# A causal mask moved from TensorE matmuls into VectorE's score maxima, in the first of four attention stages of a ten-stage network

## The reference, cut to what matters

```python
Q = (X @ W_q).reshape(b, n, H, 2 * DH).transpose(0, 2, 1, 3)   # H = 8, DH = 16, n = 256
Q1, Q2 = (Q[..., :DH], Q[..., DH:])                            # K1, K2 likewise
causal = jnp.tril(jnp.ones((n, n), jnp.bool_))
A1 = jnp.where(causal, jnp.einsum('bhqd,bhkd->bhqk', Q1, K1) * scaling, neg_inf)
A2 = jnp.where(causal, jnp.einsum('bhqd,bhkd->bhqk', Q2, K2) * scaling, neg_inf)
attn = softmax(A1, axis=-1) - lam * softmax(A2, axis=-1)
O = jnp.einsum('bhqk,bhkd->bhqd', attn, V)                     # then RMS norm, W_o, residual
```

## Time and profile before

| | |
|---|---|
| runs, us | 2519.81, 2519.93, 2523.47 |
| profiled execution, span, us | 2522.1 |
| busy, us | PE 2226.5, DVE 1726.6, ACT 1597.0, POOL 1213.1 |
| first attention stage, 30 to 437 us | 407.0: PE busy 403.0, DVE 298.8, ACT 266.5, POOL 233.2, granted TensorE clock 1.00 |

### The profile page before, as it was taken

How to read it: one execution, slowest core, us unless ns; L and a number is a source line. 1 busy time by engine, 2 the same in 40 slices (tenths; PEclk the granted TensorE clock), 3 DMA queues, 4 the chain that set the end, 5 groups by cost and what they waited for, 6 DMA issues and landing times. The chain is left out here.

```text
span 2522.1 us, 59734 instructions
## 1 busy us (share of the span) xinstructions
PE 2226.5 (88%) x19192; PEld 1631.9 (65%) x19192; DVE 1726.6 (68%) x4756; ACT 1597.0 (63%) x3564; POOL 1213.1 (48%) x1722
## 2 busy tenths in 40 slices
PE   8999998899699887999779888899698788888996
PEld 5666665699466655799666555589444455555795
DVE  6677776444578786544667888666788577886666
ACT  5666665377466665577548888544476178886444
POOL 4456665455244555455123566456411234665563
PEclk9999999899799999999879999899897989998998
DMA  8100000322300001222200000223300000001225
GB/s 284 63 6 12 13 12 11 102 67 71 80 2 6 16 15 53 79 70 64 71 5 2 9 17 18 71 67 82 97 1 1 5 2 4 17 17 55 67 79 138
DMA packets 134005, 116.57 MB, mean 46 GB/s; under 512 B 22919, under 2 KB 120213, under 8 KB 131664
## 3 DMA queue, kind: packets, MB, share of 16 engines
q1 hardware_dynamic: 116432, 78.17, 11.0%
q0 software_dynamic: 17280, 34.65, 4.2%
HBM read 58.22 MB, written 56.36 MB: 45 GB/s over the span
## 5 line engine op out<-in xcount | busy, mean ns | idle before, releaser
L1254 ACT ACTIVATE A_Pm<-A_t 128x768 f32<-128x768 f32 (+1 forms) x512 | 468.6, 915 | 157.6 <-PE A_t L1689 153.5
L371 POOL DMA_INDIRECT ybuf<-F_yo,F_idx x284 | 315.7, 1112 | 248.9 <-DVE F_yo L580 146.0
L1442 DVE TENSOR_REDUCE A_padm<-A_s 128x4 f32<-128x1024 f32 x264 | 322.7, 1222 | 66.1 <-PE A_s L1681 64.7
L225 POOL DMA_INDIRECT xbuf<-xs,dst x256 | 270.0, 1055 | 104.0 <-issue 58.4
L741 PE MATMUL F_hb<-F_xT,F_wt 128*128 128x128 f32 x2272 | 305.9, 278 | 1.0 <-issue 0.6
L1716 PE MATMUL A_ot<-A_Pm,A_V 128*32 128x256 f32 (+3 forms) x3640 | 296.8, 390 | 11.0 <-POOL A_Pm L1133 10.0
L1689 PE MATMUL A_t<-A_Q,A_K 32*128 32x256 f32 (+1 forms) x2560 | 305.9, 333 | 0.0
L1133 POOL TENSOR_SCALAR_AFFINE_SELECT A_Pm<-A_Pm 128x512 f32<-128x512 f32 x256 | 167.7, 655 | 285.6 <-ACT A_Pm L1254 284.0
L741 PEld LDWEIGHTS F_hb<-F_xT,F_wt 128*128 128x128 f32 x2272 | 275.6, 192 | 7.2 <-issue 2.4
L1681 PE MATMUL A_s<-A_K,A_Q 32*128 32x256 f32 (+1 forms) x1584 | 202.1, 332 | 60.0 <-DVE A_padm L1442 42.1
L753 PE MATMUL F_out<-F_WA,F_g 128*128 x1704 | 244.9, 280 | 6.1 <-DVE F_g L571 3.0
(11 more groups left out here) (424 smaller groups left out, 4938.6 us busy)
## 6 DMA issues: line engine op xcount, KB each, us to landing
F_xr<-xbuf SPq DMA_DIRECT2D x284, 68.0 KB, 1.9
xbuf<-A_zero SPq DMA_DIRECT2D x16, 1088.0 KB, 18.0
xs<-ybuf SPq DMA_DIRECT2D x32, 512.0 KB, 7.0
ybuf<-F_yo,F_idx POOLq DMA_INDIRECT x284, 2.5
xbuf<-xs,dst POOLq DMA_INDIRECT x256, 2.6
F_WA<-in_L_ffn_ew SPq DMA_DIRECT2D x2, 2048.0 KB, 9.2
F_WA<-in_L_ffn_ew SPq DMA_DIRECT2D x16, 256.0 KB, 5.6
F_WA<-in_L_ffn_e_gate SPq DMA_DIRECT2D x2, 1024.0 KB, 5.8
```

What stands on the lines that cost most here:

```text
L225: pool.indirect_dma_start(out=G["XBUF"][:, :], out_offset=bass.IndirectOffsetOnAxis(ap=G["dst"][:, t, c:c + 1], axis=0), in_=G["xs"][c][:, ...
L371: pool.indirect_dma_start(out=YBUF[:, :], out_offset=bass.IndirectOffsetOnAxis(ap=idx[n][:, h:h + 1], axis=0), in_=yo[r][:, h, :], in_offs ...
L1254: act.activation(Pm[r][:, j:j + 2, :], tbank[:, :].rearrange("p (j k) -> p j k", j=2)[:, :, 0:PW], ACT.Exp, scale=SCALE).then_inc(t_free, 1)
L1442: last = dve.reduce_max(tops.rearrange("p t j -> p j t"), sbank[:, :].rearrange("p (j t k) -> p j t k", j=2, t=TPS), AX)
```

## The change

For kind "diff" alone the mask matmuls, the identity in bf16 and `maskS` are gone; the `score` matmuls start their bank themselves. DVE builds once a float tile `mask3` of 384 columns (mask, zeros, mask), and `top` becomes four `tensor_tensor_reduce`: for each of the two maps one over 128 columns and one over 256. Each adds the mask to the scores from the score bank, writes the sum as bf16 to a tile that nobody reads (`masked_s`), and gives the maximum. The kind "causal" keeps its matmuls, and the other stages are as they were.

```diff
@@ -941,7 +941,10 @@
     if masked:
         mf = Pm[0][:, :, :].rearrange("p j k -> p (j k)")[:, 0:2 * P].rearrange("p (c k) -> p c k", k=P)
-        identb, maskS = sb("identb", [P, P], BF16), sb("maskS", [P, 2, P], BF16)
+        if diff:
+            mask3, masked_s = sb("mask3", [P, 3 * P]), [sb(f"masked_s{k}", [P, 2, 2, PW], BF16) for k in range(2)]
+        else:
+            identb, maskS = sb("identb", [P, P], BF16), sb("maskS", [P, 2, P], BF16)
...
@@ -1418,9 +1421,14 @@
-            if masked:
+            if masked and not diff:
                 dve.tensor_copy(identb[:, :], ident[:, :])
                 dve.tensor_copy(maskS[:, :, :], mf[:, 0:2, :])
+            if diff:
+                dve.memset(mask3[:, P:2 * P], 0.0)
+                for c in (0, 2):
+                    last = dve.tensor_copy(mask3[:, c * P:(c + 1) * P], mf[:, 0, :])
+                last.then_inc(mask_set, 1)
...
@@ -1434,10 +1442,15 @@
                 tops = padm[r][:, :, 2 * h:2 * h + 2, MROW]
-                if masked:
+                if masked and not diff:
                     two = sbank[:, :].rearrange("p (j k) -> p j k", j=2)
                     dve.reduce_max(tops[:, 0, :], two[:, :, 0:P], AX)
                     last = dve.reduce_max(tops[:, 1, :], two[:, :, P:PW], AX)
+                elif diff:
+                    for j in range(2):
+                        for t, (c, width) in enumerate(((0, P), (P, SEQ))):
+                            last = dve.tensor_tensor_reduce(masked_s[r][:, h, j, c:c + width], sbank[:, j * 512 + c:j * 512 + c + width], mask3[:, c:c + width],
+                                                            1.0, -3e38, ALU.add, ALU.max, tops[:, t, j:j + 1])
...
@@ -1679,7 +1694,7 @@
-                                     start=not masked, stop=True, skip_group_check=masked)
+                                     start=not masked or diff, stop=True, skip_group_check=masked and not diff)
```

More of the change, by code:

```diff
@@ L996, in attention_stage @@
     tail_bank = [shared[NEND % 2], shared[(NEND + 1) % 2]]
-    dense_high = sem("dense_high")
+    dense_high, mask_set = sem("dense_high"), sem("mask_set")
     if diff:
@@ L1517, in _ @@
             stat(1)
+            if diff:
+                dve.wait_ge(mask_set, 1)
             for n in range(2):
```

## The result

| | runs, us | median | to the kernel before |
|---|---|---|---|
| before | 2519.81 to 2523.47 (4) | 2521.47 | |
| changed | 2501.11 to 2511.68 (4) | 2502.49 | 0.9929 [0.9911, 0.9947] |
| changed, run again with the last experiments | 2497.28 to 2507.13 (6) | 2501.58 | 0.9924 [0.9910, 0.9938] |

The forecast was 2537 us; the change makes the kernel 19 us faster. The time is that of the rival named "faster", 2501 us, which had a chance of 0.12.

A forecast was written before the change was run, and what follows sets the result against it. PE bound the first attention stage; DVE would become the bound: 38.9 + 9.0 = 47.9, plus waits 5.0, 52.9 against 50.9 for two sequences, + 16 for eight pairs, lead-in + 1: 2537 us, range 2504 to 2580.

The forecast's parts named there:

- the rival named "faster": First attention stage: reads hide under their main parts, t near 1.05, PE stays the bound; - 19 us, 2501; chance 0.12.
- the price of the read of the maximum: DVE's four accumulator reads per half, priced by ACT's 0.09 us each, 0.36 together.
- What is added: t: t is the step of all DVE maxima of a half in the first attention stage: 0.94 before, taken as 1.50 us.
- the case in which a read waits for its main part: DVE's maxima: each read starts after its main part ends; t 1.7 to 2.2, 2565 to 2603 us; chance 0.28 with slower operation.
- The bound from below: DVE's reads cost nothing, like a one-element memset starting inside a running statistic; low end of t, 1.02.
- `weigh` of group 3: PE waits there for POOL's cut behind the root, with no slack; about 1.2 us a sequence in the faster rival.
- DVE's own work 38.7 plus small gaps: DVE over two sequences: busy 38.7 us plus gaps 1.1, less tails of eleven score waits, 38.9 before the dearer maxima.
- the break-even: The t at which time stays the same: balance for t 1.25 to 1.40, - 1 us at 1.30; chance 0.15.
- its chance of 0.76 for slower: Whole kernel slower by over 0.2%, 5 us: forecast 0.45, reads waiting or a slower operation 0.28, balance over + 5 0.03.
- POOL's root as the wait that stays: DVE's scaling of the heads still waits for POOL's reciprocal root: 3.76 - 0.60 - t, 1.7 us each, 3.3 in two sequences.
- The add of y: DVE's `add_y` waits 3.05 - t - 0.1 = 1.4 us in one sequence of two, none in the other.
- The claim that the fused operation may run at half rate: DVE's fused operation takes twice as long per element: t near 2.3, + 95 us; counted within the 0.28 for slower.

The follow-up runs named there:

- the filler run: The changed kernel with one more VectorE addition of 322 columns from the score bank before the four fused operations: 2525.44 us against 2520.84 for the kernel before, ratio 1.0022.

## Why the prediction was wrong

The step that failed is the price of the read of the maximum, in "What is added: t". The four reads were priced at 0.36 from ACT's accumulator, and t was then raised from 1.38 to 1.50, towards the case in which a read waits for its main part and for a fused operation a little dearer than an addition. The reads cost 0.05 in all, and the four main parts 1.06, where 1.02 was the sum. The bound from below, "nothing, as the one-element memset", was the right row, and it stood in the prediction with the argument against it that a memset depends on nothing. That argument is now refuted: the read depends on the result and is still shown to start in step with the next main part. The Trainium skill, VectorE: DVE Perf Modes, section "The DRAIN you can't avoid", by which the next operation waits until the pipe is empty, was given room for this read in the prediction. The same section excepts an operation that is "not held", and by the rows above neither the read nor the main part behind it is: the next main part starts 0.21 us after one that lasts 0.28.

What that one term was worth in the prediction's own sum: with t = 1.11, DVE needs 38.9 + 16 x 0.17 = 41.6 us for two sequences, less than PE's 45.9, so PE stays the bound and the rival's line holds: 45.9 + 2 x 1.2, 48.3 to 48.4, measured 48.80; 2501 us, measured 2502.5. From the forecast's 52.9 that is 4.5 less for two sequences, 36 us for sixteen, which is more than the 34.5 between forecast and result. By the runs the price of t is smaller: from the filler run at t = 1.51 to the changed kernel it is 23.6 us (+ 4.6 and - 19.0), and the rest, 11 to 12, belongs to the second failed step, below.

That the fast rival's line came so close is partly luck. PE alone needs 46.7 us and not 45.9, since the mask pair gives back 0.22 us and not 0.31 in every second half, and POOL's cut costs 1.1 + 0.8 = 1.9 in two halves (3, 0) (4.34 and 4.04 against 3.25) and not 2.4. The mechanism was right: PE bound before, the wait for `s_free` where maxima are late, as in the filler run, and `weigh` of group 3 as the place where PE's gain is given back, all show in the rows.

The second failed step is "DVE's own work 38.7 plus small gaps": it took each operation of DVE at the duration that it had beside POOL's cut as it then fell. It shows only where t is large: at the t of the forecast the time is + 4.6, not + 17. By the filler run the break-even is therefore higher than in the prediction, which had - 1 us at t = 1.30: at t = 1.51 the kernel is 0.2% slower, at 1.11 it is 0.7% faster, and a straight line between the two ends, an estimate, crosses at about t = 1.4. The durations are shown to depend on the cut; that they are the reason for all of the 12 us is worked out from the sums (1.5 us for two sequences), no run has them at t = 1.50 with the longer durations. Even with t right at 1.50 the forecast would have missed by 12 us, and its chance of 0.76 for slower rested on both errors.

POOL's root as the wait that stays was right: 1.6 us before, 2.06 now. The estimate of it from t alone (3.76 - 0.60 - t) gives 2.05 at t = 1.11. The add of y waits 1.9 where 3.05 - 1.11 - 0.1 = 1.84 was the rule. Other stages are unchanged but for the noise of one execution, and the granted clock in the stretch of two sequences is still 1.00.

The claim that the fused operation may run at half rate is refuted for these operands: 128 more columns add 0.14 us (0.35 - 0.21), 1.1 ns each, as with the plain addition.

## What to carry to other kernels

- Price an unseen short instruction of the same queue by its nearest relative on the *same* engine, and don't add for a dependency without a row that shows one. If the sign of the change hangs on that price, the range must reach to both rows and the chances must follow; here 1.02 to 2.16 was drawn, and the answer at 1.11 had been given 0.12.
- Before removing work from the busiest engine, look whether it idles: the same pair of matmuls in each half gave 27 us in this stage, where PE had no idle time, and 3.6 us in the causal one, where PE idled 34 of 311 us and its granted clock fell as well.
- When a wait stands behind a long operation (POOL's root), start its input sooner; starting it or its consumers later moves the wait to the next consumer.

## What the runs showed of the hardware

- A fused add and maximum with its accumulator read costs DVE hardly more than the add: 1.11 us for four of them with four reads, 1.06 for four plain additions.
- A VectorE operation with two operands in SBUF is held while POOL's `affine_select` on SBUF runs: 128x512 elements take 0.69 us alone and 1.11 to 1.16 when both start together, 128x32 take 0.19 and up to 0.67. Operations with an operand in the score bank are not (0.41 to 0.42 in every run; in the changed kernel 0.41 in the mean both for the 30 `with_max` beside a cut and for the others). The Trainium skill, SBUF — State Buffer, section "SBUF: two separate sides", describes it as a port pair that an operation of VectorE with two SBUF inputs and one of GpSimd that reads SBUF take in turn, the later one blocked. The traces agree: what is lost is the time to the cut's end, less 0.14 us (0.42 to 0.47 beside a cut of 0.63 that starts with it). They agree the other way round too: in the kernel before, a cut that starts at 37.88, 0.14 us after L1465 at 37.74, lasts 1.05 us instead of 0.63, and L1465 keeps its 0.68.
- POOL's power takes 2.93 us for 16 elements a partition. A product in its place shortens a sequence by 0.8 to 1.1 us, and starting the root 0.8 us earlier by 0.5 to 0.7.
- With the mask matmuls of the causal stage left out, the granted clock was 0.92 there instead of 0.98, and over the whole program 0.938 to 0.941 in four executions instead of 0.943 to 0.948.
